# A transformer block with routed experts on one core: the shared expert's output bias moves from matmuls on TensorE to adds on GpSimd, and GpSimd computes where routed rows go

## The reference

```
x = x + 0.5 * ffn(layernorm(x))
x = x + attn(layernorm(x))
x = x + 0.5 * ffn(layernorm(x))

ffn: scores = softmax(xf @ gate_w.T); 2 of 4 groups kept; top 2 of 16 experts -> weights, idx
     y = sum over the 2 experts of weight * ((silu(xf@We1+be1) * (xf@We3+be3)) @ We2 + be2)
     z = (silu(xf @ ws1 + bs1) * (xf @ ws3 + bs3)) @ ws2 + bs2
     return y + z
```

## Time and profile before

| | us |
|---|---|
| median of 3 runs | 1550.31 (1538.19 to 1560.65) |
| the profiled execution, its time | 1541.71 |
| its span, first to last instruction | 1540.0 |
| mean granted TensorE clock | 0.941 of full |

### The profile page before, as it was taken

The page is one execution under the profiler, slowest core; times in us unless marked ns, Lnnn a source line. Parts: engine busy times, 40 slices in busy tenths (PEclk is TensorE's granted clock), DMA queues, the critical chain, the costliest instruction groups (busy, mean ns, idle before and its releaser), DMA issues.

```text
span 1540.0 us, 27583 instructions
## 1 busy us (share of the span) xinstructions
PE 1273.1 (83%) x7304; PEld 991.1 (64%) x7304; DVE 917.9 (60%) x3386; ACT 678.9 (44%) x1474; POOL 575.2 (37%) x593
## 2 busy tenths in 40 slices
PE   5999777799879995999999989779777998898840
PEld 3656444587767784888888866446444887787720
DVE  5767534465556665777767656566453665555565
ACT  4444410366556662333343454434212766565500
POOL 2576454255445450000000004736542554454410
PEclk9999888899999998999999999889888999999975
DMA  9422115344434434111210001212133544444379
GB/s 383 138 88 88 59 70 114 121 144 140 121 118 134 121 103 123 55 58 60 61 57 27 1 0 57 91 49 84 69 104 100 151 146 132 122 138 119 93 285 370
DMA packets 93324, 173.08 MB, mean 112 GB/s; under 512 B 17496, under 2 KB 60525, under 8 KB 91891
## 3 DMA queue, kind: packets, MB, share of 16 engines
q1 hardware_dynamic: 63606, 93.25, 20.6%
q0 software_dynamic: 26112, 67.82, 12.5%
q10 hardware_dynamic: 3456, 10.25, 1.7%
HBM read 88.64 MB, written 86.79 MB: 114 GB/s over the span
## 4 chain that ended last, share of the span: by engine, by line
PE 64%; DVE 10%; another core or an unknown queue 7%; ACT 7%; issue 7%; DMA 3%; POOL 1%; DVEq 0%; ACTq 0%; POOLq 0%
PE bank L544 17%; PE bank L425 9%; PE bank L554 8%; PE bank L442 6%; PE bank L535 5%; PE bank L588 4%; PE bank L577 4%; PE bank L651 3%; DMA w<-routed_rows 3%; PE bank L407 2%; PE bank L556 2%; PE bank L397 2%; ACT xn L808 1%; ACT rows L713 1%
## 5 line engine op out<-in xcount | busy, mean ns | idle before, releaser
L1332 POOL DMA_INDIRECT routed_rows<-xn,rdest x288 | 283.6, 985 | 326.3 <-DVE rw L1145 208.5
L544 PE MATMUL bank<-rows 128*128 128x128 f32 x2304 | 310.2, 278 | 19.1 <-ACT rows L796 12.6
L544 PEld LDWEIGHTS bank<-rows 128*128 128x128 f32 x2304 | 280.5, 192 | 30.9 <-ACT rows L796 22.9
L1310 POOL DMA_INDIRECT expert_rows<-rows,slots x192 | 186.2, 970 | 187.0 <-DVE slots L959 113.3
L1156 DVE SCALAR_TENSOR_TENSOR rows<-bank,tile_b,rows 128x128 f32<-128x128 f32 x288 | 101.0, 351 | 225.3 <-ACT rows L801 170.6
L554 PE MATMUL bank<-w,rows 128*128 x576 | 177.5, 390 | 46.1 <-DVE rows L1156 45.8
L442 PE MATMUL bank<-ws,work 128*128 128x256 f32 x512 | 154.8, 432 | 68.9 <-DVE work L1085 30.0
L796 ACT COPY rows<-w 128x512 f32 x288 | 178.5, 620 | 15.7 <-issue 9.4
L442 PEld LDWEIGHTS bank<-ws,work 128*128 128x128 f32 x512 | 99.3, 213 | 103.3 <-DVE work L1085 33.8
L795 ACT COPY rows<-bank 128x256 f32<-128x256 f32 x288 | 106.7, 370 | 112.8 <-PE bank L535 101.8
L801 ACT ACTIVATE rows<-bank,tile_b 128x128 f32<-128x128 f32 x288 | 104.9, 364 | 81.4 <-PE bank L544 77.1
(11 more groups left out here) (184 smaller groups left out, 2155.2 us busy)
## 6 DMA issues: line engine op xcount, KB each, us to landing
rows<-expert_rows SPq DMA_DIRECT2D x288, 130.5 KB
rows<-routed_rows SPq DMA_DIRECT2D x32, 512.0 KB, 4.8
w<-routed_rows SPq DMA_DIRECT2D x10, 1024.0 KB, 19.1
out<-xres ACTq DMA_DIRECT2D x16, 512.0 KB, 7.0
xres<-in_x SPq DMA_DIRECT2D x7, 1024.0 KB, 7.7
expert_rows<-pad SPq DMA_DIRECT2D x48, 130.5 KB
rows<-routed_rows SPq DMA_DIRECT2D x6, 1024.0 KB, 16.0
routed_rows<-xn,rdest POOLq DMA_INDIRECT x288
```

The costliest lines, as they stand in the source:

```text
L544: last = nc.tensor.matmul(rh_ps[t % 2][:, n * P:(n + 1) * P], m.rw13[:, t % 2, c * C + n * INTER:c * C + (n + 1) * INTER], m.rT[:, t % 2, ...
L1310: nc.gpsimd.indirect_dma_start(out=d.xg, out_offset=bass.IndirectOffsetOnAxis(ap=m.slots[:, b % XS, k, i:i + 1], axis=0), in_=xs[:, i, :], ...
L1332: nc.gpsimd.indirect_dma_start(out=d.yt, out_offset=bass.IndirectOffsetOnAxis(ap=m.rdest[:, n:n + 1], axis=0), in_=m.ry[:, n, :], in_offse ...
```

## The change

- The bf16 bias matmul in `down` is gone. L442's second product now ends the accumulation.
- bs2 is loaded once, broadcast to all partitions (`half_bs2`), by SyncE as the first DMA of its list, and halved on GpSimd.
- GpSimd adds it to x in place: 16 adds of 128x128 for a batch, one after each scatter of batch r, to the x of batch (r + 2) mod 8. The first of these waits until that batch has been normalised (`xn_half`), or for b of 6 and 7 until the shared expert's output has been added to it (`y_added`). VectorE's `add_shared`, `combine` and the last adds wait for `bias_added`.
- `rdest` is computed on GpSimd (`place`), between the scatters of the experts stage; the scatter waits for it (`placed`), and so does SyncE before it reloads the slot.
- Two small tiles share the memory of others, to make room.

```diff
-    m.e1 = sb("e1", [P, NT, E])
+    m.e1 = m.sh
-    m.pos = sb("pos", [P, NT, E])
+    m.pos = m.ex
+    m.half_bs2 = sb("half_bs2", [P, C])
@@ load_rows (SyncE)
                     wait(sp, s.rmeta_ready, t + 1 - SLOTS)
+                    wait(sp, s.placed, t + 1 - SLOTS)
@@ SyncE, start of its list
+            sp.dma_start(m.half_bs2[:], d.biases[BS2:BS2 + C].rearrange("(o c) -> o c", o=1).to_broadcast([P, C])
+                         ).then_inc(s.bs2_in, 16)
@@ down (TensorE)
                     for mi in range(KC):
-                        nc.tensor.matmul(y_ps[t % 2][:, 0:C], m.gT[:, g, mi, t * P:(t + 1) * P],
-                                         m.ws2[:, mi, :], start=mi == 0, stop=False)
-                    nc.tensor.matmul(y_ps[t % 2][:, 0:C], m.ones3[:], m.bias_rows[:, BS2:BS2 + C],
-                                     start=False, stop=True).then_inc(s.y_ready, 1)
+                        last = nc.tensor.matmul(y_ps[t % 2][:, 0:C], m.gT[:, g, mi, t * P:(t + 1) * P],
+                                                m.ws2[:, mi, :], start=mi == 0, stop=mi == KC - 1)
+                    last.then_inc(s.y_ready, 1)
@@ add_shared (VectorE)
                 dve.wait_ge(s.y_ready, NT * r + i + 1)
+                if r % BATCHES >= 2 and i == 0:
+                    dve.wait_ge(s.bias_added, r - 1)
@@ places (VectorE)
                 ch.settle()
-                nc.vector.tensor_scalar(m.rdest[:, n:n + 1], flag[:, 1:2], float(TOKENS), r[:, C:C + 1], ALU.mult, ALU.add)
                 ch.did(nc.vector.tensor_scalar(m.rw0[:, n:n + 1], flag[:, 0:1], r[:, C + 3:C + 4], None, ALU.mult))
@@ GpSimd, route stage
+            def add_bias(r, k, i):
+                L, b = r // BATCHES, (r + 2) % BATCHES
+                q = L * BATCHES + b
+                if k == 0 and i == 0:
+                    if b < 2:
+                        pool.wait_ge(s.y_added, NT * (q + 1))
+                    else:
+                        pool.wait_ge(s.xn_half, 2 * q + 2)
+                x = m.xres[:, b, i, k * P:(k + 1) * P]
+                last = nc.gpsimd.tensor_tensor(x, x, m.half_bs2[:, k * P:(k + 1) * P], ALU.add)
+                if k == 1 and i == NT - 1:
+                    last.then_inc(s.bias_added, 1)
+
             def scatter(r, k):
                 for i in range(NT):
+                    if i or k:
+                        add_bias(r, (NT * k + i - 1) // NT, (i - 1) % NT)
                     nc.gpsimd.indirect_dma_start(
...
@@ GpSimd, experts stage
+            def place(t):
+                n = t % SLOTS
+                r, flag = m.rin[:, n, :], m.rf[:, n, :]
+                pool.wait_ge(s.rmeta_ready, t + 1)
+                wait(pool, s.rows_out[n], 16 * (t // SLOTS))
+                nc.gpsimd.tensor_scalar(m.rdest[:, n:n + 1], flag[:, 1:2], float(TOKENS), r[:, C:C + 1],
+                                        ALU.mult, ALU.add).then_inc(s.placed, 1)
+
             def experts(L):
                 for i in range(TILES):
                     t = L * TILES + i
                     n = t % SLOTS
+                    place(t)
                     pool.wait_ge(s.ry_scaled, t + 1)
-                    pool.wait_ge(s.rmeta_ready, t + 1)
+                    pool.wait_ge(s.placed, t + 1)
```

More of the change, by code:

```diff
@@ L262, in program @@
     s.pads_ready, s.padded, s.table_ready = sem("pads_ready"), sem("padded"), sem("table_ready")
+    s.bs2_in, s.bias_added, s.placed = sem("bs2_in"), sem("bias_added"), sem("placed")
     s.rows_ready, s.is_expert_ready = sem("rows_ready"), sem("is_expert_ready")
@@ L432, in down @@
                 pe.wait_ge(s.gated_ready, 4 * r + 2 * g + 2)
-                if r == 0 and g == 0:
-                    pe.wait_ge(s.bias_placed, 16)
                 if r == BATCHES and g == 0:
@@ L525, in experts @@
                 pe.wait_ge(s.tile_b13_copied, L + 1)
+                if L == 0:
+                    pe.wait_ge(s.bias_placed, 16)
                 pe.wait_ge(s.gated_ready, 4 * (BATCHES * L + 7) + 3)
@@ L1173, in combine @@
                 n = PAIRS * b + h
+                if n == 0:
+                    dve.wait_ge(s.bias_added, BATCHES)
                 y = m.ylq[:, n % YSLOTS]
@@ L1280, in _ @@
                 shared(1, n, iter(()), 0)
+            dve.wait_ge(s.bias_added, 2 * BATCHES)
             for n in range(BATCHES * PIECES):
@@ L1323, in route @@
                     scatter(r, 1)
+                    add_bias(r, 1, NT - 1)
+            def place(t):
[5 more added lines that the diff above has]
+                                        ALU.mult, ALU.add).then_inc(s.placed, 1)
             def experts(L):
@@ L1369, in _ @@
             pool.sem_inc(s.setup_done, 1)
+            pool.wait_ge(s.bs2_in, 16)
+            ch.then(nc.gpsimd.tensor_scalar(m.half_bs2[:], m.half_bs2[:], 0.5, None, ALU.mult))
             rstd(0)
```

## The result

The changed kernel took 1629.32 us (median of 4, 1626.60 to 1634.68), the kernel before beside it 1551.93. The ratio is 1.0616 (interval 1.0571 to 1.0662): 6% slower, where 1550 with a range to 1612 was forecast.

What follows compares the result with a forecast made beforehand. No engine was full; finished matmuls told late during close scatters were the loss, and GpSimd would bound the experts stage. 1541.7 - 26 + 25 = 1540.7, plus 8.6 to the median and 1 for the load: 1550, range 1520 to 1612.

Steps and rivals of the forecast that it cites:

- The term of +25: Experts stages: rdest on GpSimd adds 12.3 us in layer 0 and 13.0 in layer 1, bounds +8 to +51.
- the walk through the route stage: Route stage: following the batches through adds, waits and removed bias matmuls, experts stages begin sooner, -26 us for both layers.
- the ring: Route stage: a burst's add waits for a normalise, which waits for the previous burst's scatters to land; 29.9 us a burst.
- The threshold of 1.4 us: GpSimd: a scatter is worked off about 1.4 us after its start; one started sooner delays word of finished matmuls.
- Bounds 2.01 and 2.16, value 2.07 us a tile.: Experts stage: GpSimd's time a tile from scatter 0.98, the rdest operation 0.20 and the scatter's preparation 0.89.
- Of 17.1 us, 12.3 remain: Experts stage, layer 0: of 17.1 us more, 4.8 are covered by the shared expert's last parts beside GpSimd's scatters.
- Scatter to scatter is then 1.51.: Route stage: with an add of 0.35 us between, scatters are 1.51 us apart, 0.24 more, 3.6 us a batch.
- The burst of batch 4 ends at about 192: Route stage, layer 0: the end of batch 4's scatters comes some 21 us later, at about 192.
- Of these I count 11.: Layer 0: of silu's 19.79 us wait, 11 are saved, so the experts stage begins that much sooner.
- the hold theory: Finished matmuls are told late while scatters follow closely; about 0.3 us a tile in experts stages, gone with wider spacing.
- Rival A: Late telling of finished matmuls stays in the route stage, +13 us in layer 0, +16 in layer 1: 1604; chance 0.35.
- Rival B: Experts stage: a scatter's preparation overlaps the small operation, TensorE sets 1.65 us a tile: about 1435; chance 0.08.

Runs made afterwards that it cites:

- the third experiment: The changed kernel with GpSimd computing rdest one tile ahead of the scatter that needs it: 1473.43 us, ratio 1.0859.
- the spacer run: The kernel before with an unused 128x128 two-input add on GpSimd between any two scatters, in both stages: 1427.79 us, ratio 1.0497; on another chip 1430.07 us, ratio 0.9063.
- the memset: The kernel before with an unused memset of one column on GpSimd between any two scatters, in both stages: 1529.10 us, ratio 0.9994.
- The long spacer: The kernel before with an unused 128x128 add on GpSimd ahead of each scatter of the experts stages only: 1451.76 us, ratio 0.92; in both stages 1430.07 us.

## Why the prediction was wrong

The mechanisms were mostly the right ones. Two steps of the sum failed, both to the cheap side. The larger is the tile of the experts stage: 2.19 us and not 2.07. The term of +25 came out at +73 (39.6 + 36.4 - 3.4). The other is the walk through the route stage, in which a burst of the ring was too short, mostly for the length of its adds, and the ring was let go too early: -26 came out at +7. A further 9 us are the start of the profiled execution, +10 for +1, most of which is not of the change. These three are the 90 us between the two profiles; the medians are 77 apart, since the profiled execution of the changed kernel lies 2.5 above its median and the one before 10 below. The threshold of 1.4 us was wrong too, but did not count here, since no scatter of the changed kernel is closer than 1.64.

**"Bounds 2.01 and 2.16, value 2.07 us a tile."** It was 2.19, above both bounds. The 128x1 operation takes 0.28, not VectorE's 0.20; my upper neighbour, 0.29, was right and I took the other. The scatter grew from 0.98 to 1.03, which no bound had, and starts of instructions cost 0.03. The preparation of 0.89 was 0.85. 143 x 0.12 in two layers are 34 us. A further 10 us are tiles that waited for something else: the mean is 2.22, the median 2.19. That GpSimd becomes the bound, and that it is the wait and not the operation that costs, held; the third experiment shows it.

**"Of 17.1 us, 12.3 remain", "15.0 less 2".** About 7 us were to be covered; the parts of the sum outside route bursts and experts stages give 3.4 back.

**"Scatter to scatter is then 1.51."** It was 1.64. The add takes 0.475, not 0.35. I had 0.60 as a case, but only as 7.4 us more for a batch; that the holds depend on this distance too, I did not work out for it.

**"In this phase a burst goes: 29.9 us."** 32.4 to 32.8 us. By its terms, in the turn shown above: landing 1.99 for 1.9, normalise 4.04 as counted, add and restart 0.70 for 0.55, and 26.0 from the second scatter to the last one's end for 23.4. Of these 2.6, 2.3 are the steps (burst 5, which has no power, takes 24.4 where 22.1 was counted) and 0.3 the power. The form of the ring was right: the rows show the wait of 4.48 us in the middle of it.

**"The burst of batch 4 ends at about 192", "batches 5 to 7 take about 26 us each", "the last at 251".** Here the route term changed its sign: -26 us for both layers came out at about +7 without the start. The last burst started at 275.01, 24 us late. By the rows, 10 of these are the later first scatter, where 1 was counted. A further 15 had gathered by the end of burst 4, at 216.72, since each burst of the ring is 2.7 us longer than the 29.9. Then 6 came back, because burst 5 starts 0.66 us after burst 4 and not 7, and 6 were lost again on the last two turns, 57.6 for 52. I had written that the wait holds for r from 1 to 5, but walked with the ring only to batch 4. Burst 5 still adds to batch 7 and waits for its normalise, so the turn from burst 5 to 6 takes 30.8 us; the spacer run, which has no such wait, needs 26.8 there. The last turn, 26.8, is near the 26.

**"Of these I count 11."** The pause before the experts stages shrank by 11.4 and 11.3 us. That part of the hold theory was right, for the stage of which it spoke, and nothing was left of it because the bursts before it were longer by more.

**"128 bias matmuls are 14 us of TensorE's time. They count only where TensorE is what is waited for."** On a chip without holds they count nowhere: 0.9996. On one with holds it is not shown.

**"Two scatters 1.51 apart are hardly above 1.4"; "the backlog grows at 1.27, at 1.6 there is none".** Distance decides, as was said, but not from 1.4 on. Scatters 1.51 apart keep the holds (two runs), those 1.64 apart don't (the changed kernel's route stage, the spacer in both stages). Between these nothing was tried. At 1.51 the operation between two scatters is `rdest` and at 1.64 a 128x128 add, so the kind of operation differs as well; the memset, and no operation at all, keep the holds at 1.27.

As a sign of a time beyond the range I had named adds longer than 0.6 us. They took 0.475, and the time is beyond it all the same.

Rival A came nearest to the 1629 with 1604, by a wrong reason: it let the holds stay in the route stage. There are none; the stage is as long on a chip that has no holds at all (242.1 and 241.5 us). Rival B, a preparation that overlaps the operation, is what happens with `rdest` one tile ahead.

What I could not have read from one profile is how far the kernel before was from its own best: its 1552 us are 190 more than it takes elsewhere. Of these, by the two profiles, 87 are in the experts stages (278.9 and 281.0 against 236.4 and 236.2 us), 83 in the route bursts (225.6 and 228.2 against 184.4 and 186.3) and 20 in the pauses before the experts stages (24.3 and 23.7 against 15.0 and 13.3); its start was 9 shorter. The change takes the place of something that was partly lost already. Beside a kernel before without holds it costs 20%.

The Trainium skill's "GPSIMD Engine Reference", section "Elementwise — side-by-side cycle accounting", gave me an estimate of 0.28 us for the add before dispatch; the profile has 0.475. With it, steps would have been at 1.44, further from the 1.64 than my own.

## What to carry to other kernels

Ask of every small instruction on the engine that issues indirect DMAs whether the next DMA waits for it. A wait that is met only at that moment costs about 0.7 us more than one that was met a tile before (0.85 against 0.16), and no list of busy times shows it. Look for a ring when an edit makes an engine wait in mid-work: write down whom it waits for, what that one waits for, and whether the answer is the engine's own work; then the pace is the whole ring, for as many turns as the edit makes. And time the kernel before on more than one chip, and more than once, before you explain its profile.

## What the runs showed of the hardware that I had not expected

- The same program takes 1359 us on two chips and 1527, 1552 and 1577 in three other comparisons. In profiles taken beside the longer ones TensorE's finished matmuls are told late while scatters follow each other by 1.27 to 1.51 us; at 1.64 none is. Why this differs, whether by chip or by occasion, and what in the chip holds the messages back, no run here shows. I infer the late telling from "remote" waits and from silus that start long after their matmuls' modelled end; the runs themselves show that distance takes the lost time away.
- The long spacer takes 125 us off when it stands in the experts stages alone (1451.76 against 1576.59), and a further 22 when it stands in the route stages too (1430.07).
- A scatter mostly takes 0.96 to 1.00 us behind another scatter or behind the 128x128 add, and 1.03 behind the `rdest` operation, in every kernel that has it on GpSimd.
- A two-input add of 128x128 takes 0.44 to 0.62 us on GpSimd, 0.475 on average, and the scatter follows by 0.17 when nothing is waited for.
